# A decoder layer's cross-attention: the product with the values of every second context tile is issued one step later

## The chip, the cores and the metric

The kernel runs on one core of one Trainium2 chip. The metric is the time of one execution on the device in microseconds (us). Three runs of the kernel before gave 905.28 us as their median, with 904.61 the lowest and 910.01 the highest.

## What is computed

The reference is one layer of a decoder for 8 sequences of 112 tokens, 512 wide: self-attention with 16 heads of 128, then cross-attention to a context of 375 tokens with 32 heads of 16, then a gated mixture of experts. Only the middle part matters here:

```python
q = x @ Wq.T                                   # (8, 112, 512)
kv = concatenate([context @ Wk.T, context @ Wv.T], -1).reshape(b, 375, 32, 16, 2)
k, v = kv[..., 0], kv[..., 1]                  # per head
q, k = rmsnorm(q), rmsnorm(k)                  # over the 16 of a head
attn = softmax(q k^T / 4)                      # over the 375 context tokens
x = x + (attn @ v)                             # per head, heads side by side
x = x + ffn(layernorm(x))                      # gate needs this layernorm
```

## The kernel before, in words

The program is written out by hand: each engine has one function that issues its instructions in a fixed order, and semaphores tie the engines together. No scheduler moves anything. Matrix products in higher precision are made as three products of split halves (high and low), lines 595, 596 and 597, so these three lines stand for most of TensorE's (PE's) work.

**Passes and tiles.** The cross-attention runs in 16 passes, `u` from 0 to 15: sequence `u // 2`, and of its 32 heads the half `u % 2`. The 375 context tokens are three tiles of 125, `m` = 0, 1, 2. So there are 48 steps, `n = 3u + m`, and `keys[n]` is the pair `(u, m)`. The change calls a tile an item: the second item is `m == 1`, the third `m == 2`.

**What PE does in a step** (`step`, line 882), in its order:

- `score_pe(n)`: the scores of tile n, 16 matmuls (line 852) that each use 32 of the array's rows. It needs the transposed keys `kT` of the tile, the transposed queries `qT` of the pass, and the exponentials of the step before.
- a piece from `aside(n)`, which goes round every six steps: the transposed result of a pass (`out_pe`, line 879), a layer norm's rows transposed (`norm_turn`, line 711), or a part of the gate (`gate_pe`, lines 595 to 597 on `gw`, and 838). In the steps with `m == 2` of an even pass from 2 on it is `norm_turn(3, b - 1)`, which transposes `xn`; in those of an odd pass it is the 8-row transpose of line 838.
- `rows_pe(keys[n + 4])`: the keys and values of the tile four steps on, 12 matmuls of 512 columns, into one of two banks `KB`. In steps with `m == 0` also `rows_pe(u + 1, "q")`, the next pass's queries.
- `rows_turn(keys[n + 3])`, line 812: the normed keys of the tile three steps on, transposed.
- `value_pe(n)`, line 869: the product of the exponentials `ee` with the values `vb`, 16 matmuls with 32 columns of weights each, added up over the pass in the bank `AB`.
- in steps with `m == 1`, for all passes but the last: `queries_turn(u + 1)`, line 819, the next pass's queries transposed, into the free half of a bank `KB`.

The two banks `KB` are used in turn by tiles and queries. So `rows_pe` in a step with `m == 2` writes the bank in which `queries_turn` left the queries, and waits until VectorE (DVE) has copied them out (`q_copied`):

```python
def kb_wait(n):
    if n > 1:
        w.wait_ge(*kn_done[items[n - 2]])
        if items[n - 2][1] == "q":
            w.wait_ge(*q_copied[items[n - 2][0]])
```

**What DVE does behind `rows_turn` in a step with `m == 1`,** in its order: `k_copy` (line 1911, the transposed keys out of their bank), `rows_sum` (line 1880, needs ScalarE's squares of the rows that PE has just made), in even passes from 2 on `norm_out(3, b - 1)` (lines 1635, 1640, 1642 and 1644, the last writes `xn`), and then `q_copy` (line 1919, writes `qT` and fires `q_copied`).

**What ScalarE (ACT) does:** the exponentials (line 1377, four a step, into 8 buffers `ee`, so those of step n + 2 need the product of step n to be over), the squares (line 1357), the values' copy `vb` (line 1363, 6 buffers) and the copy of a finished pass out of `AB` (line 1383).

After step 47 PE goes on with the feed-forward part, whose first products (`up_pe(0, ...)`) already take the place of `rows_pe` in steps 44 to 47.

Of the kernel before, what the change touches and what calls it, by code (L numbers as in the profile page):

```python
# [18 lines left out]
M, MC, MS = 375, 3, 125  # L19
# [67 lines left out]
def decoder_layer(nc, x_d, ctx_d, wqk_d, wv_d, wo_d, wqx_d, wkv_d, gw_d, moe_d, wexp_d, mask_d, cst_d,  # L87
                  out_d):
    stack = ExitStack()
    with stack:  # L90
# [256 lines left out]
        def aside(n):  # L347

            b, i = n // 6, n % 6
            if i in (0, 3):  # L350
                return ("o", n // MC - 1) if n else None
            if i == 1:
                return ("n", 2, b + 1) if b + 1 < NB else None
            return (("n", 3, b - 1) if i == 2 else ("g", b - 1, i + 1)) if b else None
# [236 lines left out]
        def tensor(e):  # L591
# [183 lines left out]
            def rows_pe(u, m):  # L775
                n = at_item[u, m]
                b, hf = u // 2, u % 2
                kb_wait(n)
                if m == "q":
                    w.wait_ge(*xT_done[2][b])  # L780
                    w.wait_ge(*wqx_lo[1])
                    for k in range(KC):
                        i = mm3(KB[n % 2][0:T, 0:256], at(xT, ALL, k, toks(b * T, T)), at(wqx, ALL, k, toks(hf * 256, 256)),
                                k == 0, k == KC - 1)
                else:
                    c = ctx[(b * MC + m) % 4]
                    w.wait_ge(*ctx_lo[b * MC + m])
                    w.wait_ge(*wkv_lo[2])
                    for k in range(KC):
                        i = mm3(KB[n % 2][0:MS, :], at(c, ALL, k, ALL), at(wkv, ALL, k, hf, ALL), k == 0, k == KC - 1)  # L790
                i.then_inc(*kb_full.did((u, m)))
# [15 lines left out]
            def rows_turn(it):  # L807
                n, u = at_item[it], ("t", it)
                w.wait_ge(*kn_done[it])
                tx_free(tx_before[u])  # L810
                for g in range(2):
                    i = e.transpose(TX[u][:, g * MS:(g + 1) * MS], kn[n % 2][0:MS, g * 128:(g + 1) * 128], ident[0:MS, 0:MS])  # L812
                i.then_inc(*tx_full.did(u))

            def queries_turn(u):
                n = at_item[u, "q"]
                w.wait_ge(*kn_done[u, "q"])
                for g in range(2):
                    i = e.transpose(QT[u][:, g * T:(g + 1) * T], kn[n % 2][0:T, g * 128:(g + 1) * 128], ident[0:T, 0:T])
                i.then_inc(*q_turned.did(u))  # L820

            def norm_turn(which, b):
                u = ("n", which, b)
                w.wait_ge(*xn_done[which][b])
                tx_free(tx_before[u])
                turn_rows(TX[u], xn[0], T).then_inc(*tx_full.did(u))

            def gate_pe(b, part):
                u = ("g", b, part)
                tx_free(tx_before[u])  # L830
                if part == 5:
                    w.wait_ge(*xT_done[3][b])
                    w.wait_ge(*gw_lo[0])
                    for k in range(KC):
                        i = mm3(TX[u][0:NE, 0:T], at(gw, ALL, k, ALL), at(xT, ALL, k, toks(b * T, T)), k == 0, k == KC - 1)
                else:
                    w.wait_ge(*gl_done[b])
                    i = e.transpose(TX[u][0:T, 0:NE], lT[b % 2][:, :], ident[0:NE, 0:NE])
                i.then_inc(*tx_full.did(u))

            def score_pe(n):
                u = n // MC
                w.wait_ge(*k_copied[keys[n]])
                w.wait_ge(*q_copied[u])
                if n:
                    w.wait_ge(*x_exped[n - 1, 3])
                else:
                    for i in range(2, 6):
                        w.wait_ge(*pj_dve[pj_last[i]])
                for g in range(2):  # L850
                    for r in range(4):
                        i = e.matmul(SX[r][0:MS, g * 2 * T:(g + 1) * 2 * T], kT[n % 6][32 * r:32 * r + 32, g, :],  # L852
                                     qT[u % 2][32 * r:32 * r + 32, g, :, :], start=True, stop=True)
                        if g:
                            i.then_inc(*scored_x.did((n, r)))

            def value_pe(n):
                u, m = keys[n]
                w.wait_ge(*squared[(u, m), "v"])
                w.wait_ge(*consts_set["one", 11])  # L860
                if m == 0:
                    if u:
                        w.wait_ge(*oo_done[u - 1])
                    else:
                        w.wait_ge(*pj_dve[pj_last[6]])
                for r in range(4):
                    w.wait_ge(*x_exped[n, r])
                    for c in range(4):
                        i = e.matmul(AB[32 * c:32 * c + VW, r * T:(r + 1) * T], vb[n % 6][:, 8 * (c // 2) + 2 * r + c % 2, :],  # L869
                                     ee[(4 * n + r) % 8][:, c * T:(c + 1) * T], start=m == 0 and r == 0,  # L870
                                     stop=m == MC - 1, skip_group_check=True)
                    i.then_inc(*valued.did((n, r)))

            def out_pe(u):
                x = ("o", u)
                w.wait_ge(*oo_done[u])
                tx_free(tx_before[x])
                for r in range(4):
                    i = e.transpose(TX[x][0:T, r * 128:(r + 1) * 128], oo[u % 2][:, r * T:(r + 1) * T], ident[:, :])  # L879
                i.then_inc(*tx_full.did(x))  # L880

            def step(n):
                u, m = keys[n]
                x = aside(n)
                score_pe(n)
                if x and x[0] == "o":
                    out_pe(x[1])
                elif x and x[0] == "n":
                    norm_turn(*x[1:])
                elif x:  # L890
                    gate_pe(*x[1:])
                if n + 4 < NK:
                    rows_pe(*keys[n + 4])
                else:
                    up_pe(0, (n - NK + 4) // 2, n % 2)
                if m == 0 and u + 1 < NU:
                    rows_pe(u + 1, "q")
                if 0 < n < NK - 3:
                    rows_turn(keys[n + 3])
                value_pe(n)  # L900
                if m == 1 and u + 1 < NU:
                    queries_turn(u + 1)

# [19 lines left out]
            def up_pe(n, c, a):  # L923
                u, o = ("u", n, c, a), 0
                if n:
                    k = at_job["s", c // 2]
                    p, o = E[k % 2], WU if c % 2 else 0
                    part_wait(k, 3 if c % 2 else 0)
                else:
                    p = ring[c % 3] if c else SE  # L930
                    w.wait_ge(*s_lo[c, down_third[c] - 1])
                w.wait_ge(*xT_done[3][NB - 1 if n else 4])
                gu_wait(u)
                for k in range(KC):
                    z = o + (k * 128 if c == NS - 1 else k * 256 + a * 128)
                    i = mm3(GU[u][:, 0:SH[n]], at(p, ALL, toks(z, 128)), at(xT, ALL, k, toks(n * SH[0], SH[n])), k == 0, k == KC - 1)
                i.then_inc(*gu_full.did(u))
# [161 lines left out]
            for n in range(NK):  # L1099
                step(n)  # L1100
# [1619 lines left out]
```

## Time and profile before

| what | us |
|---|---|
| median of three runs (lowest to highest) | 905.28 (904.61 to 910.01) |
| span of the profiled execution | 905.1 |
| PE busy | 891.1 |
| DVE busy | 593.1 |
| ACT busy | 466.8 |
| POOL busy | 202.8 |

The span is the time from the first to the last instruction of one profiled execution. The trace shows weight loads on a row of their own, PEld, which overlap the matmuls (PE); a gap in PEld is where it is best seen that TensorE did not go on. In a row of the timeline the number in brackets is the idle time of that engine ahead of the row, with what ended it, or "issue" where the profile shows nothing that was waited for. A matmul's end is modelled, so it is its start that counts.

### The profile page before, as it was taken

What the parts mean: (1) busy time and instruction counts of PE and PEld (TensorE: products, weight loads), DVE (VectorE), ACT (ScalarE), POOL (GpSimd) and SP (SyncE); (2) the same over time, 40 slices, a digit from 0 to 9 for tenths busy, and PEclk for the clock granted to TensorE, in tenths of its full rate; (3) what the DMA queues carried; (4) which work ended last, traced back from release to release, by engine and by line L of the source; (5) the groups of instructions that cost most, each with busy time, mean ns of one, the idle gap of its engine ahead of it and who ended that gap; (6) DMA issues with size and microseconds to landing.
All of it is one profiled execution on the core that took longest, in us unless ns stands there. A gap on an engine that the chain in (4) does not pass through costs nothing.

```text
span 905.1 us, 17929 instructions
## 1 busy us (share of the span) xinstructions
PE 891.1 (98%) x7088; PEld 778.4 (86%) x7088; DVE 593.1 (66%) x1304; ACT 466.8 (52%) x1119; POOL 202.8 (22%) x147
## 2 busy tenths in 40 slices
PE   9999999999999999999999999999999999999995
PEld 8998989898989898877777787778777898999994
DVE  7886565757575635775655655646457878888882
ACT  5543333343434344647666666666575336656561
POOL 0143232323333225201101101011000621232322
PEclk9999999999999999999999999999999999999998
DMA  6221232324212115140201001000043687999973
GB/s 223 65 93 41 89 128 94 123 93 123 94 53 94 41 47 180 35 129 23 64 10 36 23 15 36 13 24 13 1 164 124 246 301 301 350 288 315 286 194 47
DMA packets 42195, 104.56 MB, mean 116 GB/s; under 512 B 8208, under 2 KB 18560, under 8 KB 40192
## 3 DMA queue, kind: packets, MB, share of 16 engines
q1 hardware_dynamic: 37808, 94.23, 30.7%
q0 software_dynamic: 4304, 9.19, 5.3%
q8 instruction: 56, 0.92, 0.4%
q14 instruction: 27, 0.22, 0.1%
HBM read 75.57 MB, written 18.65 MB: 104 GB/s over the span
## 4 chain that ended last, share of the span: by engine, by line
PE 79%; DMA 13%; POOL 3%; issue 2%; DVE 2%; ACT 1%; SPq 0%; POOLq 0%; DVEq 0%
PE bank L595 20%; PE bank L596 19%; PE bank L597 19%; DMA out<-yg,meta 11%; PE bank L852 5%; PE bank L869 5%; PE bank L695 3%; PE bank L671 2%; POOL out L2437 1%; PE bank L711 1%; DMA ctx_f<-ctx 1%; PE bank L812 1%; PE bank L683 1%; PE bank L879 1%; POOL wkv_lo L2327 1%
## 5 line engine op out<-in xcount | busy, mean ns | idle before, releaser
L1377 ACT ACTIVATE ee<-bank 125x448 f32<-125x448 f32 x192 | 91.2, 548 | 28.8 <-PE bank L852 28.8
L1625 DVE TENSOR_TENSOR E_lo<-F,E_hi 128x940 fp32r<-128x940 f32 (+3 forms) x62 | 80.8, 1321 | 2.1 <-ACT E_hi L1144 2.0
L595 PE MATMUL bank<-wkv_hi,ctx_hi 128*125 128x512 f32 x192 | 80.0, 417 | 0.3 <-DVE kn L1902 0.3
L2327 POOL TENSOR_TENSOR ctx_lo<-ctx_f,ctx_hi 128x500 fp32r<-128x500 f32 x24 | 30.6, 1275 | 208.1 <-ACT ctx_hi L1144 208.1
L596 PE MATMUL bank<-wkv_hi,ctx_lo 128*125 128x512 f32 x192 | 76.1, 396 | 0.0
L597 PE MATMUL bank<-wkv_lo,ctx_hi 128*125 128x512 f32 x192 | 75.7, 394 | 0.0
L1144 ACT ACTIVATE E_hi<-F 128x940 fp32r<-128x940 f32 (+3 forms) x62 | 67.9, 1140 | 6.8 <-PE bank L597 3.6
L2327 POOL TENSOR_TENSOR wqk_lo<-wqk_f,wqk_hi 128x1024 fp32r<-128x1024 f32 x14 | 35.1, 2508 | 155.7 <-ACT wqk_hi L1144 155.7
L2437 POOL DMA_INDIRECT out<-yg,meta x21 | 38.5, 1832 | 129.4 <-DMA out<-yg,meta 87.8
L1911 DVE COPY kT<-bank 128x250 f32<-128x250 f32 x48 | 20.1, 418 | 69.0 <-PE bank L812 68.8
L595 PE MATMUL bank<-wv_hi,xT_hi 128*128 128x256 f32 x224 | 63.4, 283 | 0.1
L597 PE MATMUL bank<-wv_lo,xT_hi 128*128 128x256 f32 x224 | 62.5, 279 | 0.0
L596 PE MATMUL bank<-wv_hi,xT_lo 128*128 128x256 f32 x224 | 62.5, 279 | 0.0
L1144 ACT ACTIVATE wshi<-wqk_f 128x1024 fp32r<-128x1024 f32 x12 | 12.7, 1060 | 87.8 <-DVE wqk_f L1682 87.8
L595 PE MATMUL bank<-E_hi,xgT_hi 128*128 128x352 f32 x168 | 56.5, 337 | 0.2 <-DVE E_lo L1625 0.2
L597 PE MATMUL bank<-E_lo,xgT_hi 128*128 128x352 f32 x168 | 54.2, 323 | 0.0
L596 PE MATMUL bank<-E_hi,xgT_lo 128*128 128x352 f32 x168 | 54.1, 322 | 0.0
L1357 ACT ACTIVATE sq<-bank 125x256 f32<-125x256 f32 (+1 forms) x64 | 24.6, 384 | 56.5 <-PE bank L597 56.0
L852 PE MATMUL bank<-qT,kT 32*125 32x224 f32 x768 | 49.8, 373 | 0.0
L1763 DVE TENSOR_TENSOR xa<-xa,bank 128x512 f32<-128x512 f32 x56 | 37.7, 685 | 17.7 <-PE bank L597 17.3
L1223 ACT ACTIVATE pp<-sm,nm 112x112 f32<-112x112 f32 x128 | 47.7, 378 | 0.0
L869 PE MATMUL bank<-ee,vb 125*32 125x112 f32 x1536 | 46.8, 262 | 0.0
(411 smaller groups left out, 2569.7 us busy)
## 6 DMA issues: line engine op xcount, KB each, us to landing
F<-wexp SPq DMA_DIRECT2D x14, 1408.0 KB, 8.3
F<-wexp SPq DMA_DIRECT2D x14, 768.0 KB, 7.8
wqk_f<-wqk SPq DMA_DIRECT2D x16, 512.0 KB, 4.4
ctx_f<-ctx SPq DMA_DIRECT2D x24, 250.0 KB, 2.7
slots<-zt SPq DMA_DIRECT2D x3, 1799.0 KB, 8.3
xg<-slots SPq DMA_DIRECT2D x21, 256.0 KB, 7.6
wv_f<-wv SPq DMA_DIRECT2D x8, 512.0 KB, 5.4
wo_f<-wo SPq DMA_DIRECT2D x8, 512.0 KB, 3.5
```

The source lines that it names most:

```text
L595: e.matmul(out, a[0], b[0], start=first, stop=False)
L596: e.matmul(out, a[1], b[0], start=False, stop=False)
L597: return e.matmul(out, a[0], b[1], start=False, stop=last)
L852: i = e.matmul(SX[r][0:MS, g * 2 * T:(g + 1) * 2 * T], kT[n % 6][32 * r:32 * r + 32, g, :], qT[u % 2][32 * r:32 * r + 32, g, :, :], start= ...
L869: i = e.matmul(AB[32 * c:32 * c + VW, r * T:(r + 1) * T], vb[n % 6][:, 8 * (c // 2) + 2 * r + c % 2, :], ee[(4 * n + r) % 8][:, c * T:(c + ...
L1144: return e.activation(out, src, ACT.Copy)
L1223: i = e.activation(pp[g][:, c, :], sm[g][:, c, :], ACT.Exp, bias=nm[g][:, c:c + 1], scale=ISQ, accum_out=rs[g][:, c:c + 1])
L1377: e.activation(ee[(4 * n + r) % 8][:, :], SX[r][0:MS, 0:4 * T], ACT.Exp, scale=0.25).then_inc(*x_exped.did((n, r)))
L1625: return e.tensor_tensor(out, src, high.bitcast(F32), ALU.subtract)
L1763: e.tensor_tensor(xa[:, j, :], xa[:, j, :], PJ[u][:, :], ALU.add).then_inc(*pj_dve.did(u))
L2327: return e.tensor_tensor(out, src, high.bitcast(F32), ALU.subtract)
L2437: e.indirect_dma_start(out_d, bass.IndirectOffsetOnAxis(ap=meta[:, unit_of[j], 0:1].bitcast(U32), axis=0), yg[j % 4][:, :], None, compute_ ...
```

## The change

In a step with `m == 1` PE no longer issues `value_pe(n)`. In the step behind it, with `m == 2`, it issues `value_pe(n - 1)` right ahead of `value_pe(n)`. Nothing is added or removed, and no other engine's order changes.

```diff
                 if 0 < n < NK - 3:
                     rows_turn(keys[n + 3])
-                value_pe(n)
+                if m == MC - 1:
+                    value_pe(n - 1)
+                if m != 1:
+                    value_pe(n)
                 if m == 1 and u + 1 < NU:
                     queries_turn(u + 1)
```

TensorE's order at the end of a step with `m == 1` and at the start of the next (pass 0, steps 1 and 2; `L812` is `rows_turn`, `L869` the product with the values, `L819` `queries_turn`, `L852` the scores of step 2). Before:

```order
L597 MATMUL bank<-wkv_lo,ctx_hi 125x512
L812 MATMUL bank<-ident,kn_143 128x125 x2
L869 MATMUL bank<-ee_166,vb_145 32x112 x4
L869 MATMUL bank<-ee_167,vb_145 32x112 x4
L869 MATMUL bank<-ee_168,vb_145 32x112 x4
L869 MATMUL bank<-ee_169,vb_145 32x112 x4
L819 MATMUL bank<-ident,kn_142 128x112 x2
L852 MATMUL bank<-qT_170,kT_152 125x224 x8
L595 MATMUL bank<-wkv_hi,ctx_hi 125x512
```

and now:

```order
L597 MATMUL bank<-wkv_lo,ctx_hi 125x512
L812 MATMUL bank<-ident,kn_143 128x125 x2
L819 MATMUL bank<-ident,kn_142 128x112 x2
L852 MATMUL bank<-qT_170,kT_152 125x224 x8
L595 MATMUL bank<-wkv_hi,ctx_hi 125x512
```

The four groups of the product with `vb_145` are gone from between the two transposes, so that the queries' transpose follows the keys' at once.

TensorE's order at the end of the step with `m == 2` (step 2). Before:

```order
L812 MATMUL bank<-ident,kn_143 128x125 x2
L869 MATMUL bank<-ee_162,vb_146 32x112 x4
L869 MATMUL bank<-ee_163,vb_146 32x112 x4
L869 MATMUL bank<-ee_164,vb_146 32x112 x4
L869 MATMUL bank<-ee_165,vb_146 32x112 x4
L852 MATMUL bank<-qT_171,kT_153 125x224 x8
L879 MATMUL bank<-ident,oo_172 112x128 x4
```

and now:

```order
L812 MATMUL bank<-ident,kn_143 128x125 x2
L869 MATMUL bank<-ee_166,vb_145 32x112 x4
L869 MATMUL bank<-ee_167,vb_145 32x112 x4
L869 MATMUL bank<-ee_168,vb_145 32x112 x4
L869 MATMUL bank<-ee_169,vb_145 32x112 x4
L869 MATMUL bank<-ee_162,vb_146 32x112 x4
L869 MATMUL bank<-ee_163,vb_146 32x112 x4
L869 MATMUL bank<-ee_164,vb_146 32x112 x4
L869 MATMUL bank<-ee_165,vb_146 32x112 x4
L852 MATMUL bank<-qT_171,kT_153 125x224 x8
L879 MATMUL bank<-ident,oo_172 112x128 x4
```

The moved groups stand here, with the same operands, and the two products of the pass are one run of eight groups.

## Rows read from the trace of the kernel before

**Rows 1.** The page: busy time of TensorE, and the granted clock in 40 slices.

```profile
PE 891.1 (98%) x7088; PEld 778.4 (86%) x7088; DVE 593.1 (66%) x1304; ACT 466.8 (52%) x1119; POOL 202.8 (22%) x147
PEclk9999999999999999999999999999999999999998
```

**Rows 2.** What weight loads waited for: us in total, times, longest.

```profile
PEld bank L869 <- issue: 8.2, 47, 0.4
PEld bank L711 <- DVE xn L1644: 2.2, 8, 0.3
PEld bank L595 <- DVE qT L1919: 1.6, 8, 0.3
```

**Rows 3.** Timeline of weight loads, pass 5: end of m = 1, start of m = 2.

```profile
493.66 0.38 PEld L812 LDWEIGHTS bank<-ident,kn 125*128 125x128 f32 x2
494.19 0.73 PEld L869 LDWEIGHTS bank<-ee,vb 125*32 125x32 f32 x32 [0.16 <-issue]
495.10 0.20 PEld L819 LDWEIGHTS bank<-ident,kn 112*128 112x128 f32 x2 [0.17 <-issue]
495.44 0.69 PEld L852 LDWEIGHTS bank<-qT,kT 32*125 32x125 f32 x16
496.11 0.13 PEld L838 LDWEIGHTS bank<-ident,lT 8*112 8x112 f32 x1
496.41 0.18 PEld L595 LDWEIGHTS bank<-wkv_hi,ctx_hi 128*125 128x125 f32 x1 [0.17 <-DVE qT L1919]
```

**Rows 4.** Timeline of VectorE in the same stretch.

```profile
494.30 0.42 DVE L1911 COPY kT<-bank 128x250 f32<-128x250 f32 x1 [2.99 <-PE bank L812]
494.64 0.41 DVE L1880 TENSOR_REDUCE ss<-sq 125x16 f32<-125x256 f32 x1
495.55 0.62 DVE L1919 TENSOR_TENSOR qT<-bank,half 128x448 f32<-128x448 f32 x1 [0.50 <-PE bank L819]
```

**Rows 5.** Timeline of weight loads, pass 6: m = 1, then start of m = 2.

```profile
508.36 0.39 PEld L711 LDWEIGHTS bank<-ident,xn 112*128 112x128 f32 x4 [0.28 <-issue]
...
511.38 0.37 PEld L812 LDWEIGHTS bank<-ident,kn 125*128 125x128 f32 x2
511.91 0.73 PEld L869 LDWEIGHTS bank<-ee,vb 125*32 125x32 f32 x32 [0.16 <-issue]
512.82 0.20 PEld L819 LDWEIGHTS bank<-ident,kn 112*128 112x128 f32 x2 [0.17 <-issue]
513.16 0.69 PEld L852 LDWEIGHTS bank<-qT,kT 32*125 32x125 f32 x16
514.12 0.39 PEld L711 LDWEIGHTS bank<-ident,xn 112*128 112x128 f32 x4 [0.28 <-DVE xn L1644]
514.55 0.18 PEld L595 LDWEIGHTS bank<-wkv_hi,ctx_hi 128*125 128x125 f32 x1
```

**Rows 6.** Timeline of VectorE in the same stretch of pass 6.

```profile
512.02 0.42 DVE L1911 COPY kT<-bank 128x250 f32<-128x250 f32 x1 [1.50 <-PE bank L812]
512.36 0.41 DVE L1880 TENSOR_REDUCE ss<-sq 125x16 f32<-125x256 f32 x1
512.68 0.32 DVE L1635 SCALAR_TENSOR_TENSOR rt<-rstd 112x1 f32<-112x1 f32 x1
...
513.42 0.55 DVE L1644 TENSOR_SCALAR xn<-xs,mv,rstd 112x512 f32<-112x512 f32 x1
513.88 0.62 DVE L1919 TENSOR_TENSOR qT<-bank,half 128x448 f32<-128x448 f32 x1
```

**Rows 7.** Timeline of ScalarE in pass 6, m = 1: last exponentials.

```profile
509.73 1.00 ACT L1377 ACTIVATE ee<-bank 125x448 f32<-125x448 f32 x2
```

**Rows 8.** Timeline of VectorE, then of weight loads: a hand-over that TensorE waited for.

```profile
391.30 0.42 DVE L1902 TENSOR_TENSOR kn<-bank,rr 112x256 f32<-112x256 f32 x1
391.78 0.20 PEld L819 LDWEIGHTS bank<-ident,kn 112*128 112x128 f32 x2 [0.29 <-DVE kn L1902]
```

**Rows 9.** Timeline of weight loads, last pass: end of m = 1, start of m = 2.

```profile
672.04 0.19 PEld L597 LDWEIGHTS bank<-xT_lo,S1hi 128*128 128x128 f32 x1
672.59 0.73 PEld L869 LDWEIGHTS bank<-ee,vb 125*32 125x32 f32 x32 [0.36 <-issue]
673.50 0.69 PEld L852 LDWEIGHTS bank<-qT,kT 32*125 32x125 f32 x16 [0.17 <-issue]
```

## The prediction

> **What bounds the kernel now.** I read the page first: TensorE is busy 891.1 of 905.1 us, at its full granted clock in nearly every slice [rows 1]. So a microsecond that TensorE loses or gains is one of the kernel's, and other engines matter only where TensorE waits for them. Next the list of waits, for the weight loads [rows 2]. The longest entry that the change touches is no wait for an engine: 8.2 us in 47 pieces ahead of the product with the values, put down to "issue". Two entries name DVE: `xn` ahead of line 711 (8 times, 2.2 us) and `qT` ahead of line 595 (8 times, 1.6 us). Last, the timeline at the place of the change, for an odd pass [rows 3, 4] and for an even one [rows 5, 6].
>
> Two things are to be seen there. First, gaps of fixed size stand wherever the array goes over between its ways of working: 0.16 us from full-height transposes to the 32-column product, 0.17 from that to transposes, 0.28 from the 32-row scores to full height. The 0.28 ahead of line 711 in pass 6 is put down to `xn`, but the same 0.28 stands one step earlier where nothing is waited for [rows 5], and `xn` was done at 513.42 + 0.55 = 513.97, 0.15 us before the load at 514.12. Likewise `qT` in pass 5 was done at 496.17, 0.24 before the load at 496.41 [rows 3, 4]. These two "waits" are gaps with DVE just in time. Second, how just: a true hand-over takes about 0.06 us (`kn` done at 391.72, load at 391.78) [rows 8]. In pass 6 `qT` is done at 513.88 + 0.62 = 514.50 and line 595 loads at 514.55, 0.05 later [rows 5, 6]: that one TensorE does wait for already. So between `rows_turn` and `rows_pe` two chains run side by side, TensorE's and DVE's, and they are almost equally long. The change shortens one of them.
>
> **TensorE's own chain, shortened.** Times are counted from the first load of line 812 (R: 493.66 in pass 5, 511.38 in pass 6). Before, in both passes: line 819 loads at R + 1.44, the scores at R + 1.78, what follows them at R + 2.74 or 2.75. The product takes 0.73 of it (32 loads), with 0.16 ahead and 0.17 behind; with it gone both transposes are of one kind and I take no gap between them. Freed: 0.73 + 0.16 + 0.17 = 1.06. The scores could load at R + 0.72, and what follows at R + 1.69. Their own inputs are there: the exponentials of the step end at 510.73, R - 0.65 [rows 7].
>
> **DVE's chain, not shortened.** It starts at `rows_turn`, whose place does not move: `k_copy` at R + 0.64, `rows_sum` at R + 0.98 [rows 4, 6].
>
> - *Odd passes, and pass 0, which has no `norm_out` here: 8.* DVE stood idle 0.50 us for line 819 ahead of `q_copy` [rows 4]. That goes. Starts on DVE are 0.33 apart, so `q_copy` starts at R + 1.31, ends at R + 1.93, and `rows_pe` loads at R + 1.99 with the hand-over. TensorE wanted R + 1.69, so it now truly waits 0.30. Before it loaded at R + 2.75: 0.76 earlier now.
> - *Even passes from 2 to 14: 7.* The small norm instructions and `xn` stand between, and DVE shows no idle ahead of `q_copy` [rows 6]: nothing can move. `xn` ends at R + 2.59, so line 711 loads at R + 2.65 against R + 2.74 before. `q_copy` ends at R + 3.12, so `rows_pe` loads at R + 3.17 or 3.18: where it loaded before (514.55 is R + 3.17). TensorE idles away all of the 1.06 us: 0.96 in front of line 711 and the rest behind it.
>
> **The product, paid later.** At the end of the step with m = 2 it stands behind `rows_turn` and in front of another product of its kind. Within a product 32 loads with four waits take 0.73 us without a gap, so I take 0.73 for 32 more and no gap; 0.16 to 0.17 is the most a gap would add. Nothing covers it, since TensorE is the bound there. Its inputs are long ready, and what waits for it has room: the exponentials that reuse its `ee` come after the next scores, the `vb` it frees is wanted a step later, and the pass's copy out of `AB` waited for the product of m = 2 anyway, which keeps its place right ahead of the scores.
>
> **The last pass (15).** There is no `queries_turn`. Before, 0.36 + 0.73 + 0.17 us lie between the last load of `up_pe` and the scores (672.23 to 673.50, 1.27 with rounding) [rows 9]. Now about 0.17 lies there, and 0.73 comes later: about 0.36 saved.
>
> **The sum.**
>
> - even passes: 7 x (0.73 - 0.00) = +5.1
> - pass 0 and odd passes: 8 x (0.73 - 0.76) = -0.2
> - last pass: -0.4
>
> That is +4.5 us on the span of 905.1, so 909.6. The median of the runs is 0.2 above this execution's span: **909.8 us**.
>
> The bounds of what the trace doesn't show: a gap between the two products or between the two transposes adds nothing at the least and 0.17 each at the most. Between the transposes it would be hidden in every pass by the wait behind it. Between the products 16 x 0.17 = 2.7 us. The hand-over in the 8 passes could be as short as 0 or as long as the 0.24 seen from `qT` to the load in pass 5, -0.5 or +1.4 us. In the even passes line 711 could be what sets `rows_pe` and not `qT`: 7 x 0.1 = -0.7. So the mechanism alone gives 908.6 to 913.9.
>
> [...]
>
> **The rivals.**
>
> - *The gaps are saved and DVE keeps up: faster, 899.9 us.* 15 x (0.16 + 0.17) + 0.36 = 5.3 us less. It speaks for it that DVE is busy 66% only [rows 1]. It needs `q_copy` to end by R + 1.63 in place of R + 1.93 and 3.12. Against it: the rows of DVE stand start to start in the even passes, from `rows_turn` on. It decides at the point where DVE's chain is shorter than 1.69 us. Chance 0.05. [...]
> - *A wash: about 905.3 us.* The even passes lose only what the gaps had cost, for instance because DVE gets its norm instructions in earlier or because TensorE, waiting in the step with m = 2, has a wait less later. For it: the scores come 1.06 us earlier, so ACT starts the exponentials earlier. Against it: no later place in a pass shows a wait above the fixed 0.28, so there is nothing to win back. Chance 0.14.
> - *Both kinds of pass pay: 914.4 us.* A gap of 0.17 stands between the two products in all 16 passes (+2.7) and the hand-over of `qT` costs 0.24 more in the 8 others than I take (+1.9, so that they lose too). Chance 0.13.
>
> My forecast has 0.68.
>
> **How the numbers follow.** About 1% (9 us) is what a measurement of this kernel can tell from no change; the three runs themselves spread over 5.4 us. The forecast, the wash and the costlier case mostly lie within it (896.2 to 914.3). Slower by over 1% needs the third rival in full or something unseen: 0.07. Faster by over 1% needs more than the first rival gives: 0.01. Same: 0.92. The range of 904.0 to 914.0 takes in the wash and nearly all of the costlier case, and leaves out the first rival and the edges.
>
> **What would show each step.** In the profile after: in the seven even passes an idle of about 1.2 us (0.28 + 0.96) ahead of line 711's loads, put down to `xn`; in the eight others 0.45 to 0.6 us ahead of line 595, put down to `qT`; DVE's 0.50 of idle ahead of `q_copy` gone in the latter and its times from `rows_turn` unchanged in the former; 64 loads of line 869 in 1.46 us without a gap; the list of waits with 31 or 32 entries for line 869 in place of 47. The forecast is wrong if line 711 loads well before R + 2.6 in the even passes, if a gap stands between the two products, or if a wait turns up in the steps with m = 0.

## The result

The changed kernel took 910.99 us as the median of 11 runs (909.53 to 915.57), against 905.28 us. The ratio is 1.006, with a 95% interval of 1.0043 to 1.0077, so 3.9 to 7.0 us more. The forecast was 909.8 us, within 904.0 to 914.0. The move makes the kernel 0.6% slower.

The page of the changed kernel, span and the first part:

```profile
span 908.4 us, 17913 instructions
PE 887.5 (98%) x7088; PEld 778.1 (86%) x7088; DVE 593.1 (65%) x1304; ACT 465.7 (51%) x1119; POOL 204.5 (23%) x147
PEclk9999999999999999999999999999999999999998
```

TensorE's clock is as before and its instructions are the same in number. What it waited for, from the list of waits of the weight loads (us in total, times, longest; lines from 903 on stand 3 further down in this kernel):

```profile
PEld bank L711 <- DVE xn L1647: 8.5, 8, 1.2
PEld bank L869 <- issue: 5.4, 31, 0.4
PEld bank L595 <- DVE qT L1922: 3.8, 8, 0.6
```

Against [rows 2]: the wait for `xn` rose from 2.2 to 8.5 us, that for `qT` from 1.6 to 3.8, and the gaps ahead of line 869 fell from 8.2 us in 47 to 5.4 in 31. Weight loads in pass 5, the place of [rows 3]:

```profile
494.67 0.37 PEld L812 LDWEIGHTS bank<-ident,kn 125*128 125x128 f32 x2
495.01 0.25 PEld L819 LDWEIGHTS bank<-ident,kn 112*128 112x128 f32 x2
495.40 0.69 PEld L852 LDWEIGHTS bank<-qT,kT 32*125 32x125 f32 x16
496.07 0.13 PEld L838 LDWEIGHTS bank<-ident,lT 8*112 8x112 f32 x1
496.64 0.18 PEld L595 LDWEIGHTS bank<-wkv_hi,ctx_hi 128*125 128x125 f32 x1 [0.44 <-DVE qT L1922]
```

and in pass 6, the place of [rows 5], up to the end of the step with m = 2:

```profile
512.36 0.38 PEld L812 LDWEIGHTS bank<-ident,kn 125*128 125x128 f32 x2
512.71 0.25 PEld L819 LDWEIGHTS bank<-ident,kn 112*128 112x128 f32 x2
513.09 0.69 PEld L852 LDWEIGHTS bank<-qT,kT 32*125 32x125 f32 x16
515.00 0.40 PEld L711 LDWEIGHTS bank<-ident,xn 112*128 112x128 f32 x4 [1.22 <-DVE xn L1647]
515.53 0.18 PEld L595 LDWEIGHTS bank<-wkv_hi,ctx_hi 128*125 128x125 f32 x1
...
518.17 0.37 PEld L812 LDWEIGHTS bank<-ident,kn 125*128 125x128 f32 x2
518.70 1.50 PEld L869 LDWEIGHTS bank<-ee,vb 125*32 125x32 f32 x64 [0.16 <-issue]
```

VectorE there, the place of [rows 6]:

```profile
513.01 0.42 DVE L1914 COPY kT<-bank 128x250 f32<-128x250 f32 x1 [1.50 <-PE bank L812]
...
514.40 0.55 DVE L1647 TENSOR_SCALAR xn<-xs,mv,rstd 112x512 f32<-112x512 f32 x1
514.86 0.62 DVE L1922 TENSOR_TENSOR qT<-bank,half 128x448 f32<-128x448 f32 x1
```

With R as the first load of line 812, `rows_pe` loads at R + 1.97 in pass 5 (R + 2.75 before) and at R + 3.17 in pass 6 (R + 3.17 before): nothing was won in pass 6, though the scores load at R + 0.73 and not R + 1.78.

The span rose by 3.3 us only, the median by 5.7. The cleanest measure of the change in one profiled execution is the stretch from the first scores to the last weight load, since it leaves out how early a given execution reached the cross-attention (0.5 us earlier in the changed kernel) and what came behind the last load (11.3 us before, 10.1 in the changed kernel). "Stretch" below is this: 500.03 us before (393.74 to 893.77), 505.02 in the changed kernel (393.25 to 898.27), so +4.99.

### The profile page after: what moved, and what is told of

It reads as the page before. It is cut to its first block, busy times and chain, and to the rows that moved or that the text cites. A ratio compares the mean times of both kernels' runs of the same rounds, so it can differ in the third digit from the quotient of the medians.

```text
span 908.4 us, 17913 instructions
## 1 busy us (share of the span) xinstructions
PE 887.5 (98%) x7088; PEld 778.1 (86%) x7088; DVE 593.1 (65%) x1304; ACT 465.7 (51%) x1119; POOL 204.5 (23%) x147
## 4 chain that ended last, share of the span: by engine, by line
PE 93%; DVE 4%; issue 1%; DMA 1%; ACT 0%; POOL 0%; SPq 0%; DVEq 0%
PE bank L595 25%; PE bank L596 24%; PE bank L597 24%; PE bank L869 5%; PE bank L852 4%; PE bank L695 3%; PE bank L671 3%; PE bank L683 1%; PE bank L711 1%; PE bank L812 1%; PE bank L981 1%; PE bank L879 1%; PE bank L989 1%; DMA xa<-x 1%; DVE ss L1883 1%
## 5 line engine op out<-in xcount | busy, mean ns | idle before, releaser
L852 PE MATMUL bank<-qT,kT 32*125 32x224 f32 x768 | 49.8, 373 | 0.0
L595 PEld LDWEIGHTS bank<-wkv_hi,ctx_hi 128*125 128x125 f32 x192 | 35.7, 186 | 12.7 <-DVE qT L1922 3.8
```

The costliest lines, as they stand in the source:

```text
L595: e.matmul(out, a[0], b[0], start=first, stop=False)
```

## The experiments

Theory: the cost is that VectorE's chain behind `rows_turn` does not move, so that TensorE waits for `xn` and `qT` in the time that it freed. Main rival: two products side by side cost something of their own, in every pass. All ratios are against the kernel before, run on the same chip. A "change of mode" in the expectations is a place where TensorE's weight loads go over between full height, 32 rows and 32 columns; ahead of the moved product and behind it the gaps at such places are 0.16 and 0.17 us [rows 3].

**The move in pass 0 and the odd passes only.**

```diff
-                if m == MC - 1:
+                late = u % 2 or u == 0
+                if m == MC - 1 and late:
                     value_pe(n - 1)
-                if m != 1:
+                if m != 1 or not late:
                     value_pe(n)
```

> The product is moved in pass 0 and the odd passes only (9 of 16, the last among them). Theory (VectorE's chain behind rows_turn does not move): in eight of these TensorE wins back by the earlier rows_pe what the product costs later, in the last it wins some 0.15 us, so the time is that of before within 0.5 us, 905.1; rows_pe loads at R + 1.98 in the odd passes (R is the first load of line 812) and at R + 3.17 in the untouched even ones. Rival (two products one behind the other cost something of their own, in each pass alike): 9/16 of the loss seen, +3, 908.3.

Measured: 905.08 us, ratio 1.000 (0.999 to 1.0011); the stretch is 499.87, 0.16 less than before. In pass 5 `rows_pe` loads at R + 1.97 as in the changed kernel. This is what the theory says; a price of the pairing would have shown in nine passes.

**The move in the seven even passes only** (`late = u % 2 == 0 and u > 0`).

> The product is moved in the seven even passes from 2 to 14 only. Theory: each loses the full product, 0.75 us, since xn and qT come no earlier: +5.2, 910.5, with an idle of 1.2 us ahead of line 711 in seven steps and none new ahead of line 595. Rival (a price of the two products standing together): 7/16 of the loss, +2.5, 907.8.

Measured: 910.83 us, ratio 1.006 (1.0047 to 1.0073), stretch +5.30. The list of waits of its weight loads has the whole new wait for `xn`, while that for `qT` is back at the 1.6 us of before:

```profile
PEld bank L711 <- DVE xn L1648: 8.5, 8, 1.2
PEld bank L869 <- issue: 7.1, 40, 0.4
PEld bank L595 <- DVE qT L1923: 1.6, 8, 0.3
```

Seven passes carry the whole loss.

**`q_copy` ahead of `rows_sum` on VectorE, in pass 0 and the odd passes,** on the changed kernel.

```diff
                 if n + 3 < NK:
                     k_copy(*keys[n + 3])
+                early = m == 1 and u + 1 < NU and not (i == 1 and b)
+                if early:
+                    q_copy(u + 1)
                 if m and n + 4 < NK:
                     rows_sum(*keys[n + 4])
...
-                if m == 1 and u + 1 < NU:
+                if m == 1 and u + 1 < NU and not early:
                     q_copy(u + 1)
```

> The changed kernel, and q_copy goes ahead of rows_sum on VectorE in pass 0 and the odd passes only. Theory: rows_pe loads at R + 1.70 in place of R + 1.98 there, even passes as in the changed kernel: 8 x 0.27 = 2.2 less than the changed kernel, 908.8. Rival (the exponentials behind rows_sum's root come later and give it back): 911.

Measured: 908.90 us, ratio 1.0035 (1.0021 to 1.0049), stretch 502.87, 2.15 less than the changed kernel. In pass 5 the wait shrinks to the fixed gap and `rows_pe` loads at R + 1.69:

```profile
494.05 0.37 PEld L812 LDWEIGHTS bank<-ident,kn 125*128 125x128 f32 x2
...
495.74 0.18 PEld L595 LDWEIGHTS bank<-wkv_hi,ctx_hi 128*125 128x125 f32 x1 [0.17 <-DVE qT L1922]
```

**The norm's rows ahead of `k_copy`, in the even passes,** on the changed kernel.

```diff
+                if i == 1 and b:
+                    norm_out(3, b - 1)
                 if n + 3 < NK:
                     k_copy(*keys[n + 3])
                 if m and n + 4 < NK:
                     rows_sum(*keys[n + 4])
-                if i == 1 and b:
-                    norm_out(3, b - 1)
```

> The changed kernel, and VectorE makes the norm's rows (line 1644 and its three small instructions) ahead of k_copy in the steps with m = 1 of even passes, where it idles 1.5 us; q_copy stays last. Theory: line 711 loads at R + 1.70 with the fixed gap of 0.28, k_copy starts 0.4 later, q_copy ends at R + 2.31, rows_pe loads at R + 2.37 in place of 3.17: 7 x 0.8 = 5.6 less than the changed kernel, 905.4, the time of before. Rival (a price of the two products together): no gain, 911.

Measured: 909.76 us, ratio 1.0045 (1.0032 to 1.0058), stretch 503.91. A miss: 1.2 us won and not 5.6. Weight loads of pass 6, with R at 512.54:

```profile
514.87 0.39 PEld L711 LDWEIGHTS bank<-ident,xn 112*128 112x128 f32 x4 [0.91 <-DVE xn L1647]
515.66 0.18 PEld L595 LDWEIGHTS bank<-wkv_hi,ctx_hi 128*125 128x125 f32 x1 [0.40 <-DVE qT L1922]
```

Line 711 loads at R + 2.33 and not 1.70, `rows_pe` at R + 3.12 where it had loaded at R + 3.17. It is the same in six of the seven even passes: `xn` takes 1.43 us in place of 0.55. Only in pass 14 does it take 0.55, and that pass alone is 0.94 us shorter than in the changed kernel. The next experiment shows why.

**Both orders together:** norm's rows, `k_copy`, `q_copy`, `rows_sum`, on the changed kernel.

> The changed kernel, and in the steps with m = 1 VectorE makes the norm's rows first, then k_copy, then q_copy, then rows_sum. Theory: no step with m = 2 waits for VectorE any more; rows_pe loads at R + 1.70 in pass 0 and the odd passes and at about R + 2.12 in the even ones. The two saved changes of mode then show: 15 x 0.28 and 0.15 less than before, 900.9. Rival (a price of the two products together): not below before, 905 or more.

Measured: 905.30 us, ratio 0.9999 (0.9991 to 1.0008), stretch +0.20. A miss again, by 4.4 us. The median alone would have spoken for the rival; the rows do not: `rows_pe` loads at R + 1.69 in pass 5, as expected, and at R + 2.80 in pass 6, where 2.12 was. Timeline of VectorE in pass 6, then POOL's, then the weight loads':

```profile
511.37 0.16 DVE L1645 SCALAR_TENSOR_TENSOR rstd<-rt,rstd 112x1 f32<-112x1 f32 x1
511.57 1.43 DVE L1647 TENSOR_SCALAR xn<-xs,mv,rstd 112x512 f32<-112x512 f32 x1
512.92 0.41 DVE L1914 COPY kT<-bank 128x250 f32<-128x250 f32 x1
```

```profile
511.47 1.25 POOL L2330 TENSOR_TENSOR ctx_lo<-ctx_f,ctx_hi 128x500 fp32r<-128x500 f32 x1 [24.11 <-ACT ctx_hi L1147]
```

```profile
511.11 0.37 PEld L812 LDWEIGHTS bank<-ident,kn 125*128 125x128 f32 x2
...
513.44 0.39 PEld L711 LDWEIGHTS bank<-ident,xn 112*128 112x128 f32 x4 [0.91 <-DVE xn L1647]
513.91 0.18 PEld L595 LDWEIGHTS bank<-wkv_hi,ctx_hi 128*125 128x125 f32 x1
```

`xn` took 1.43 us where it had taken 0.55 [rows 6]. It started 0.10 us behind POOL's `ctx_lo`, and ended 0.28 behind POOL's end (512.72). So it was, within 0.01 us, in all six even passes in which POOL makes a `ctx_lo` there. In pass 14 POOL does nothing, and VectorE's rows of the same kernel are

```profile
656.29 0.55 DVE L1647 TENSOR_SCALAR xn<-xs,mv,rstd 112x512 f32<-112x512 f32 x1
656.76 0.41 DVE L1914 COPY kT<-bank 128x250 f32<-128x250 f32 x1
```

with the first load of line 595 (in pass 14 that of `up_pe`, which stands in the place of `rows_pe`) at R + 2.05. The step that failed in both expectations is that the norm's rows would fit where VectorE idles: it left out POOL. In all six places where both work, `xn`, the second to start, took 1.42 or 1.43 us against 0.55 in pass 14. It ended only 0.28 us after POOL, less than its own 0.55, so the rows do not show all of its work held back until POOL's end, and no run shows by what the two hinder each other.

**The same with the norm's root made ahead of the exponentials on ScalarE,** so that `xn` can start before POOL.

```diff
                 for it in new:
                     rows_root(*it)
+                if i == 1 and n > 6:
+                    norm_root(3, n // 6 - 1, T)
                 score_exp(n, 0)
...
-                if i == 1 and n > 6:
-                    norm_root(3, n // 6 - 1, T)
```

> The kernel with the move and the new order on VectorE (norm's rows, k_copy, q_copy, rows_sum), and in the steps with m = 1 of even passes ScalarE makes the norm's root ahead of the exponentials, where it idles 0.52 us. That kernel gained nothing because xn took 1.43 us where it ran at the same time as POOL's ctx_lo (six passes) and 0.55 in pass 14, where POOL does nothing. Theory (VectorE's xn is held up by POOL's instruction): the root comes 2.4 us earlier, xn starts some 0.2 us ahead of ctx_lo at about R - 0.35, takes 0.55 us again, line 711 loads at R + 1.70 and rows_pe at R + 2.1 in even passes: 7 x 0.7 less than that kernel, 900.9. Rival (xn is slow wherever it stands ahead of k_copy, or TensorE finds another wait): 905 as before.

Measured: 899.90 us, ratio 0.9938 (0.9925 to 0.9952), stretch 495.11, -4.92 to before. Timeline of pass 6, VectorE, POOL and the weight loads:

```profile
509.30 0.55 DVE L1647 TENSOR_SCALAR xn<-xs,mv,rstd 112x512 f32<-112x512 f32 x1
509.60 1.35 POOL L2330 TENSOR_TENSOR ctx_lo<-ctx_f,ctx_hi 128x500 fp32r<-128x500 f32 x1 [23.70 <-ACT ctx_hi L1147]
509.66 0.37 PEld L812 LDWEIGHTS bank<-ident,kn 125*128 125x128 f32 x2
...
511.36 0.39 PEld L711 LDWEIGHTS bank<-ident,xn 112*128 112x128 f32 x4 [0.28 <-issue]
511.70 0.19 PEld L595 LDWEIGHTS bank<-wkv_hi,ctx_hi 128*125 128x125 f32 x1
```

`xn` starts 0.3 us ahead of POOL, takes 0.55 again, and POOL's instruction is the one that grows, from 1.25 to 1.35. Line 711 loads at R + 1.70 behind the fixed 0.28, `rows_pe` at R + 2.04. The places came out as expected; the total of the expectation is a slip (7 x 0.7 less than 905.3 is 900.4, not 900.9), and the stretch is 5.12 less than that of the kernel with both orders. This kernel is faster than the kernel before and than the changed one.

**The early root with `q_copy` still behind `rows_sum`,** on the changed kernel.

> The changed kernel with norm's rows ahead of k_copy and the early root, q_copy still behind rows_sum. Theory: xn at 0.55 us, q_copy ends at R + 1.93 in all passes, rows_pe loads at R + 1.98 in pass 0 and the odd ones as in the changed kernel and at R + 2.1 in the even ones in place of 3.17: 7 x 1.05 = 7.3 less than the changed kernel, 903.6. Rival (xn slow ahead of k_copy anyway): 909.8, as without the early root.

Measured: 902.70 us, ratio 0.9971 (0.996 to 0.9981), stretch 497.43, 7.59 less than the changed kernel for 7.3 expected. Pass 5 keeps its R + 1.97, and pass 6 has R + 2.04.

**The orders alone, the product not moved.** Two controls: VectorE's new order, and that with the early root.

> VectorE's new order (norm's rows, k_copy, q_copy, rows_sum) on the kernel before, the product not moved. Theory: before, TensorE's own chain was the longer one but for 0.05 us in six even passes, so the order alone gives 0.3 us, 905.0. Rival (the order is what gains, the move has nothing to do with it): 901.

Measured: 905.06 us, ratio 0.9995 (0.9986 to 1.0004).

> The same orders on VectorE and ScalarE, the product not moved. Theory: TensorE's own chain with the product in it sets rows_pe (R + 2.75, in even passes R + 3.15), so the orders alone give nothing: 905.0. Rival (they alone bring the gain): 901.

Measured: 905.03 us, ratio 0.9997 (0.9988 to 1.0006). Neither order is worth a measurable time while TensorE's own chain is the longer one: in pass 6 of the first control line 711 still loads at R + 2.75, and `rows_pe` at R + 3.10 in place of 3.17. The 5 us come from the move and the orders together.

**A move at another place:** the product of m = 0 made in the step with m = 1.

```diff
-                value_pe(n)
+                if m == 1:
+                    value_pe(n - 1)
+                if m:
+                    value_pe(n)
```

> A move of the same kind at another place: the product of m = 0 is made in the step with m = 1, right ahead of that step's own; m = 2 as before. Theory: the same law, TensorE frees 0.90 us (the product and one change of mode) ahead of rows_pe in the step with m = 1, which there waits for kn (done at 508.30 in pass 6, rows_pe loads at 508.70; 490.34 and 490.99 in pass 5). So even passes win 0.34 and odd ones 0.59 of it, and each pays 0.77 later: 8 x 0.43 + 8 x 0.18 = +4.9, 910.2, with a wait for kn (line 1902) of 0.4 to 0.6 us ahead of line 595. Rival (moving to a step without queries_turn is free of waits): one change of mode a pass saved, 903.

Measured: 910.51 us, ratio 1.0059 (1.0045 to 1.0073), stretch +5.34. Its weight loads waited

```profile
PEld bank L595 <- DVE kn L1905: 7.9, 15, 1.2
```

and in pass 6

```profile
509.83 0.18 PEld L595 LDWEIGHTS bank<-wkv_hi,ctx_hi 128*125 128x125 f32 x1 [0.51 <-DVE kn L1905]
```

The same happens with another tile: TensorE comes early to something that VectorE has not finished. The total came out close in part because two misses cancel. Passes 0, 1 and 14 lose 0.75 to 0.78 us each, all of the product, since their `kn` had been just in time; the other even passes lose 0.27 to 0.39 and not 0.43.

## Why the prediction was right

**The reading that the waits named in [rows 2] were gaps with VectorE just in time** held. It is what carried the forecast: with the chain of TensorE cut by 1.05 us, the same two names became true waits at once.

**VectorE's chain does not move.** Within 0.03 us of the forecast: in pass 6 `xn` ends at R + 2.59 and line 711 loads at R + 2.64 (R + 2.65 forecast); in pass 5 `rows_pe` loads at R + 1.97 (R + 1.99). The scores load at R + 0.73 (R + 0.72). The idle ahead of line 711 is 1.22 us (1.24), that ahead of line 595 in pass 5 is 0.44 (0.47). In pass 14 the way is slightly different from the forecast's: `up_pe` stands there in the place of `rows_pe`, so that only `xn` holds TensorE up (line 711 at R + 2.48), and `up_pe` loads at R + 3.08, against 3.10 before.

**The sum,** from the lengths of the passes between their first scores:

| term | forecast | in the trace |
|---|---|---|
| seven even passes | +5.1 | +5.2 |
| pass 0 and the odd passes, eight | -0.2 | 0.0 |
| last pass | -0.4 | -0.15 |
| together | +4.5 | +5.0 |

The lengths bear out the mechanism pass by pass: each of the seven even passes is 0.65 to 0.78 us longer, and none of the eight others changes by more than 0.02. Two small terms were mis-sized. The second product takes 0.77 us and not 0.73 (64 loads in 1.50), with no gap between the two, as taken. And in the last pass I took 0.17 us for the gap between `up_pe` and the scores. It is 0.36:

```profile
677.24 0.69 PEld L852 LDWEIGHTS bank<-qT,kT 32*125 32x125 f32 x16 [0.36 <-issue]
```

so only the gap of 0.17 us behind the product is saved there. I had read the 0.36 of [rows 9] as belonging to line 869; it stands behind `up_pe`, ahead of the product there and ahead of the scores here.

Of the 5.7 us between the medians the stretch gives 5.0. The other 0.7 lies within the interval of the ratio (3.9 to 7.0), and no run tells what it is. In the ten other kernels the change of the median and that of the stretch differ by up to 0.7 us as well, in either direction, so it need not be an effect of the move.

The range, 904.0 to 914.0, proves little by itself: it holds the time of a kernel that was not changed at all. It also doesn't take in the costlier case, as the prediction says it nearly does: that one stands at 914.4. It is the rows that decide.

**The first rival** (the gaps are saved, 899.9 us) did not come, since VectorE did not keep up. Once it was made to, with the orders of both engines changed, the kernel took 899.90. That the two numbers agree to a tenth is partly luck: between the medians lie 5.4 us, but the stretch is 4.92 shorter where the rival had 5.3. The rival took the second product at 0.73 us and 0.36 for the last pass, and measured are 0.77 and 0.2. The gaps it counts on stand in the rows before, 0.16 us from the transposes into the 32-column product and 0.17 out of it [rows 3], and none stands between two products in the changed kernel (64 loads in 1.50 us). **The wash** needed a place where the early scores help; none appeared. **Both kinds of pass pay** is refuted by the 64 loads without a gap and by the kernel that moves pass 0 and the odd passes only, at 905.08.

## What to carry to other kernels

Before work is moved off the bounding engine's path, lay the other engine's chain beside it from their last common point, and see which arrives first: here 1.05 us was freed, and VectorE's chain was 0.3 us longer than what was left of TensorE's in eight passes and 0.8 to 1.1 us longer in seven. A wait in the profile that has the same size with and without its named releaser, as the 0.28 us ahead of line 711 [rows 5], is a fixed gap, and says only that the releaser is in time by now. And a change that loses by itself may be half of one that wins: with VectorE's and ScalarE's order fitted to it, the same move made the kernel 0.6% faster, while those orders alone gave nothing.

## What the hardware showed that was not expected

- VectorE's `xn` (an instruction from SBUF to SBUF, 112 x 512) took 1.43 us in place of 0.55 when POOL's subtraction in SBUF had started 0.10 us ahead of it; it ended 0.28 or 0.29 us after POOL's end each of six times. Where VectorE was first by 0.3 us, POOL's instruction grew by 0.10 us. The kernel before shows a trace of it already: the first small instruction of the norm took 0.32 us [rows 6] while POOL was at work until 512.98 (0.26 to 0.33 in the six even passes with a `ctx_lo` there), and 0.15 in pass 14, where POOL does nothing. Not everything on VectorE took longer: `k_copy`, out of PSUM, took 0.42 us and `rows_sum` 0.41 in both places. POOL in pass 6, then VectorE in pass 14, both before:

```profile
511.73 1.25 POOL L2327 TENSOR_TENSOR ctx_lo<-ctx_f,ctx_hi 128x500 fp32r<-128x500 f32 x1 [24.41 <-ACT ctx_hi L1144]
```

```profile
656.27 0.42 DVE L1911 COPY kT<-bank 128x250 f32<-128x250 f32 x1 [2.40 <-PE bank L812]
656.60 0.41 DVE L1880 TENSOR_REDUCE ss<-sq 125x16 f32<-125x256 f32 x1
656.93 0.15 DVE L1635 SCALAR_TENSOR_TENSOR rt<-rstd 112x1 f32<-112x1 f32 x1
```

- The gap where the weight loads go over between full height, 32 rows and 32 columns was not the same everywhere. Ahead of the product it was 0.16 us behind the transposes of line 812 and 0.36 behind `up_pe`; ahead of the scores it was 0.17 behind the product and 0.36 behind `up_pe`; behind the 32-row scores it was 0.28. It does not stand at every such place, as the prediction has it: none is visible from those scores to the 8-row transpose of line 838 [rows 3].
